# Moving three elementwise passes per image from VectorE to ScalarE in the convolution stage of a four-layer network

## What is computed

```python
# layer 0: five Newton-Schulz steps towards the inverse of every 128x128 channel image
x = x + _L0_conv_ref(_gn(x), 5)
# layer 1: 3x3 convolution of the quantised input
x = x + _L1_conv_ref(_gn(x), L1_conv_weight_int8, L1_conv_scale_weight, L1_conv_bias)
# layer 2: 5-tap diagonal convolution;  layer 3: 3x3 convolution on a torus
x = x + _L2_conv_ref(_gn(x), L2_conv_filter_w)
x = x + _L3_conv_ref(_gn(x), L3_conv_weight)

# the quantisation of layer 1
scale_input = jnp.max(jnp.abs(x_cl)) / 2.0 ** (ACTBIT - 1)
x_q = jnp.round(jnp.clip(x_cl / scale_input, -n, n))        # n = 127
```

## Time and profile before

| | us |
|---|---|
| median of 3 runs | 4286.94 |
| lowest and highest run | 4285.88 and 4287.16 |
| profiled execution: its span, first to last instruction | 4285.7 |
| start of the second stage's first matmul in that span | 2277.1 |

### The profile page before, as it was taken

How to read it: one execution, slowest core, us unless ns; L and a number is a source line. 1 busy time by engine, 2 the same in 40 slices (tenths; PEclk the granted TensorE clock), 3 DMA queues, 4 the chain that set the end, 5 groups by cost and what they waited for, 6 DMA issues and landing times. The chain is left out here.

```text
span 4285.7 us, 81705 instructions
## 1 busy us (share of the span) xinstructions
PE 4194.6 (98%) x30409; PEld 3108.7 (73%) x30409; DVE 3444.2 (80%) x7393; ACT 2072.5 (48%) x4296; POOL 2407.9 (56%) x3149
## 2 busy tenths in 40 slices
PE   7999999999999999999996999999999999999998
PEld 7999999999999999999992444444444444444443
DVE  6888888888888888888876787878787888888784
ACT  5776777777777777777761222222222222222221
POOL 6888888888888888888871222222222222222221
PEclk9999999999999999999997999999999999999999
DMA  2221222222222222222214555555555555555553
GB/s 69 64 62 55 65 65 60 60 60 60 60 66 65 60 63 68 60 60 60 60 41 97 133 137 134 137 133 137 134 138 134 138 134 138 134 138 134 138 134 84
DMA packets 333657, 404.28 MB, mean 94 GB/s; under 512 B 23088, under 2 KB 286032, under 8 KB 316880
## 3 DMA queue, kind: packets, MB, share of 16 engines
q1 hardware_dynamic: 308688, 334.25, 30.8%
q10 hardware_dynamic: 24576, 64.79, 5.6%
HBM read 135.22 MB, written 134.22 MB: 63 GB/s over the span
## 5 line engine op out<-in xcount | busy, mean ns | idle before, releaser
L1392 PE MATMUL bank<-xn,wt 128*128 128x512 f16 (+1 forms) x6912 | 1661.6, 381 | 19.9 <-issue 10.7
L1164 POOL TENSOR_TENSOR xn<-F,xn 128x512 f16<-128x512 f32 x512 | 541.6, 1090 | 1453.2 <-ACT xn L1202 1453.2
L1392 PEld LDWEIGHTS bank<-xn,wt 128*128 128x128 f16 (+1 forms) x6912 | 672.9, 100 | 805.0 <-issue 21.9
L463 ACT ACTIVATE P<-bank 128x512 f32<-128x512 f32 x1024 | 606.8, 608 | 264.0 <-PE bank L962 154.5
L1266 DVE SCALAR_TENSOR_TENSOR x<-bank,wu,x 128x512 f32<-128x512 f32 x512 | 382.4, 747 | 313.7 <-PE bank L1399 306.6
L1202 ACT ACTIVATE xn<-F 128x2048 f16<-128x2048 f32 x128 | 244.9, 1913 | 603.3 <-DVE F L1322 603.3
L1399 PE MATMUL bank<-xh,wth 96*128 96x512 f16 (+1 forms) x1792 | 515.6, 380 | 12.1 <-DMA xh<-xn 12.1
L313 POOL TENSOR_TENSOR W<-W 128x512 f16<-128x512 f32 x256 | 290.3, 1166 | 145.7 <-ACT W L489 145.7
L1277 DVE BATCH_NORM_STATS2 bs<-x 128x6 f32<-128x512 f32 x512 | 355.6, 695 | 17.7
L569 DVE BATCH_NORM_STATS2 st<-X 128x6 f32<-128x256 f32 x1024 | 351.5, 411 | 5.8 <-DMA X<-in_x 5.7
L1399 PEld LDWEIGHTS bank<-xh,wth 96*128 96x128 f16 (+1 forms) x1792 | 174.2, 97 | 232.6 <-DMA xh<-xn 15.7
(11 more groups left out here) (129 smaller groups left out, 7619.3 us busy)
## 6 DMA issues: line engine op xcount, KB each, us to landing
X<-in_x SPq DMA_DIRECT2D x64, 1024.0 KB, 4.8
x_scratch<-X SPq DMA_DIRECT2D x64, 1024.0 KB, 5.6
X<-x_scratch SPq DMA_DIRECT2D x64, 1024.0 KB, 8.8
out<-x SPq DMA_DIRECT2D x64, 1024.0 KB, 3.9
xh<-xn SPq DMA_DIRECT2D x384, 131.8 KB, 4.5
xh<-xn ACTq DMA_DIRECT2D x384, 131.8 KB, 5.4
xh<-xn SPq DMA_DIRECT2D x192, 65.9 KB, 3.2
xh<-xn ACTq DMA_DIRECT2D x192, 65.9 KB, 2.7
```

The source lines that it names most:

```text
L463: nc.scalar.activation(into[:, 4 * q:4 * q + 4, :], banks[q][:, :].rearrange("p (m w) -> p m w", m=4), ACT.Copy).then_inc(sb, 1)
L1164: ins = nc.gpsimd.tensor_tensor(padded(xn[l][odd], 1)[:, a + 1:a + 5, L:L + H], F[l][:, a:a + 4, :], padded(xn[l][odd], 0)[:, a + 1:a + 5, ...
L1392: nc.tensor.matmul(bank, wt[l][:, a, k, :], v, start=(k == a == b == 0), stop=False)
```

## The change

- F of layers 2 and 3 is computed by ACT (in `upper`, ahead of the f16 copy, on the same engine) as r * x + nb instead of by DVE as (x - m) * r. DVE computes the column nb = -m * r, of width 1, in `normalise`, and a new semaphore `scale_set` takes it to ACT. F -> copy is now a wait of ACT for itself.
- The first pass of the quantisation, T, is computed by ACT in a new function `quotients` as acol * x + ncol; DVE's `quantise` waits for it (semaphore `quotient`) and does the other two passes. `quotients(s+1)` stands in ACT's order behind `halos(3, s-2)` and ahead of `root(2, s)`.
- ncol = -mcol * acol is computed once, at the end of the first stage.

```diff
+ncol = persistent("ncol", [H, B])
...
 link.done(nc.vector.tensor_scalar(acol[:, :], acol[:, :], inv[:, 0:1], None, ALU.mult))
 link.wait()
+link.done(nc.vector.scalar_tensor_tensor(out=ncol[:, :], in0=mcol[:, :], scalar=-1.0, in1=acol[:, :],
+                                         op0=ALU.mult, op1=ALU.mult))
+link.wait()
...
+def quotients(n, h, odd):
+    act.wait_ge(x1_in[odd], 16 * h + 16)
+    need(act, normed[1], n)
+    nc.scalar.activation(T[:, :, :], xs[1][odd][:, :, :], ACT.Identity, scale=acol[:, n:n + 1],
+                         bias=ncol[:, n:n + 1]).then_inc(quotient, 1)
 def upper(l, n, odd):
+    act.wait_ge(scale_set[l], n + 1)
+    need(act, normed[l], n)
+    nc.scalar.activation(F[l][:, :, :], xs[l][odd][:, :, :], ACT.Identity, scale=cols[l]["r"][:, 0:1],
+                         bias=cols[l]["nb"][:, 0:1]).then_inc(scaled_f[l], 1)
     act.wait_ge(scaled_f[l], n + 1)
     nc.scalar.activation(padded(xn[l][odd], 0)[:, 1:NJ + 1, L:L + H], F[l][:, :, :],
                          ACT.Copy).then_inc(high[l], 1)
...
     halos(3, s - 2, odd)
+if there(s + 1):
+    quotients(s + 1, h + odd, 1 - odd)
 if there(s):
     root(2, s)
     upper(2, s, odd)
...
+quotients(0, 0, 0)
 first(0, 0, 0)
 run(act, step)
...
 def quantise(n, h, odd):
-    dve.wait_ge(x1_in[odd], 16 * h + 16)
-    link = Link(dve, q_chain, 2 * n)
-    link.done(nc.vector.tensor_scalar(T[:, :, :], xs[1][odd][:, :, :], mcol[:, bass.ds(n, 1)],
-                                      acol[:, bass.ds(n, 1)], ALU.subtract, ALU.mult))
-    link.wait()
+    dve.wait_ge(quotient, n + 1)
+    link = Link(dve, q_chain, n)
     link.done(nc.vector.tensor_scalar(T[:, :, :], T[:, :, :], QMAX, MAGIC, ALU.min, ALU.add))
...
 def normalise(l, n, odd):
-    need(dve, normed[l], n)
...
     link.done(nc.vector.tensor_tensor(c["r"][:, :], c["ra"][:, :], c["rb"][:, :], ALU.mult))
     link.wait()
-    nc.vector.tensor_scalar(F[l][:, :, :], xs[l][odd][:, :, :],
-                            c["m"][:, 0:1], c["r"][:, 0:1], ALU.subtract,
-                            ALU.mult).then_inc(scaled_f[l], 1)
+    nc.vector.tensor_scalar(c["nb"][:, :], c["r"][:, :], c["m"][:, 0:1], -1.0, ALU.mult,
+                            ALU.mult).then_inc(scale_set[l], 1)
```

More of the change, by code:

```diff
@@ L1077, in conv_net @@
             PART = 512 // 2
-            cols = [None, None] + [{k: sb(f"{k}{l}", [H, 1]) for k in ("m", "s", "q", "ve", "sd", "ra", "rb", "r")}
+            cols = [None, None] + [{k: sb(f"{k}{l}", [H, 1]) for k in ("m", "s", "q", "ve", "sd", "ra", "rb", "r", "nb")}
                                    for l in (2, 3)]
@@ L1087, in conv_net @@
             q_chain = sem("q_chain")
+            quotient = sem("quotient")
+            scale_set = [None, None] + [sem(f"scale_set{l}") for l in (2, 3)]
             biased = sem("biased")
```

## The result

| | before | changed |
|---|---|---|
| median, lowest to highest run, us | 4287.05, 4285.88 to 4288.18 (4 runs) | 4384.49, 4383.02 to 4385.93 (4 runs) |
| span of the profiled execution, us | 4285.7 | 4382.4 |

The change makes the kernel slower: the ratio is 1.0228, with a 95% interval from 1.0213 to 1.0242. The forecast was 4374 us, in a range from 4345 to 4405.

What follows compares the result with a forecast made beforehand. PE bound the old kernel at 30.525 us a step; the chain, grown to 31.96, becomes the bound: +1.43 over 61 steps is +87, span 4373, plus 1.2 gives 4374 us, range 4345 to 4405.

Steps and rivals of the forecast that it cites:

- the chain through ACT, POOL and DVE: Second stage's steady steps: image rounds chained through three engines, closing each step; 25.77 us before, 31.96 after, above PE's 29.97.
- Its length: Chain in a steady step: 18.76 us for the first half and 13.20 for the second, together 31.96 us.
- The issues as a part of the chain: ACT's queue in both halves: DMA issues hold ACT up, so 3.3 us of each `halos` belong to the chain.
- DVE's relief is all that counts: Rival: ACT computes while its queue issues DMAs, the chain loses up to 6.7 us; 4253 us at best; chance 0.04.
- PE's need: PE in a steady step: 30.525 us less its 0.55 wait for DVE's `s`, so 29.97 us.
- DVE's idle time for the quotient: Sign of being right: DVE idle about 3 us for the quotient, which starts as layer 3's halo issue ends.
- No fall of the clock: PE's steady steps: waits split into pieces of about 1 us keep the clock; rival, falling clock, 4682 us, chance 0.03.
- Halos in time: Layer 2's halos in steady steps: 7.5 us to issue and land, 8.2 to 9.6 available, so free.
- the 4.75 us of the chain: Steady step before the change: chain of 25.77 us in a step of 30.525, leaving 4.75 us to spare.

Runs made afterwards that it cites:

- quotient early: Changed kernel with the quotient of image s+2 moved behind `upper(3)`, where ACT waits for POOL: 4271.20 us, ratio 0.9962 to the kernel before.
- without the issues: Changed kernel with ScalarE's half of the `halos` DMAs issued from SyncE's queue: 4276.78 us, ratio 0.9976 to the kernel before.
- PE kept busy: Changed kernel with quotient done twice in place, plus 14 unread PE matmuls ahead of the wait for layer 3's `s`: 4520.27 us, against 4561.54 without them.

## Why the prediction was right, step by step

- *That the chain through ACT, POOL and DVE becomes the bound* was right. The trace shows it link by link, and three runs that shorten it in different ways (without the quotient, with the quotient early, without the issues) end at the same 4271 to 4277 us.
- *Its length*, forecast at 31.96 us, is 32.12; 0.16 us over 61 steps are the 10 us between forecast and result. Most of it is nb, the one width-1 column that DVE computes: from the reciprocal to F's start on ACT takes 1.21 us instead of 1.14, twice in a step, since nb takes 0.21 where a width-1 operation at 0.16 was assumed. Another 0.04 is the quotient's start, 3.42 behind the first issue where the root had 3.38. F and quotient were sized right: both have 2.09, for 2.10.
- *The issues as a part of the chain* was right, against the idle time that the list of waits puts down to `ve`: in the changed kernel both quotient and root follow the last issue by about 0.1 us, and in the kernel that issues from SyncE's queue the quotient stands 3.4 us nearer to `wrap`. The rival "DVE's relief is all that counts" became true there. It was described rightly, but its gain was priced too high: 4253 us at best, where the runs stop at 4271.
- *PE's need* was the term mis-sized in that price: 29.97 us, from the wait of 0.55 that the load engine shows. With no such wait left a step takes 30.19 (quotient early). The wait of the weight load, 0.55, held PE's stream up by only 0.33. The forecast does not suffer by it, since the chain, and not PE, sets its length.
- *A bound is missing from it.* The prediction compares the chain with PE's need alone. The kernel with only the quotient shows a third round, through PE, DVE's residuals and ACT, that is longer than both (30.98 us reckoned, against 30.1 and 30.2). In the changed kernel this round stays about 1.2 us short of the chain, the time for which DVE waits for ACT's root ahead of `normalise(3)` (1.18 and 1.23 in the rows above). That it did no harm here is luck: nothing in the prediction tests it.
- *DVE's idle time for the quotient* was given as about 3 us and is 4.89. The figure left the chain's new phase out; nothing else rested on it.
- *No fall of the clock*, at waits for both `s` of about 1 us each on the weight load, some 2 us a step as forecast, was right: 1.00 in the steady stretch. The rival was not empty, though: 2 us more in the chain call it up. There what the Trainium skill ("TensorE: Matmul & The Clock Gate", section "HAM oscillation — how this bites in real kernels") tells of a PE that waits between bursts agrees in kind with the trace, which shows the clock of 0.78 and 0.58 behind the wait; the waits that it tells of are longer than the 2.5 us here.
- *Halos in time*: of the 15.0 us for which PE waited for halos by the page, 1.4 lie between 2400 and 4280, so in the steady steps they stayed free.

## What to carry to other kernels

Before you move work to an idle engine, look for the place in its program: on an engine that works in order, with DMA issues and waits for others between its operations, a pass costs its full length if it stands on a chain that closes in each iteration and sets its pace, and nothing if it fills a wait for another engine. Add up the chain around one iteration, with DMA issues as busy time of the engine that issues them, and compare it with the bound engine's need; the difference is the most that may be added. Do the same for every other round that shares links with this chain: the quotient alone stayed within the 4.75 us of the chain and cost 27 us by the round through PE. Here the same three passes cost 97 us with the quotient in one place and gained 16 with it in the other, and the gain came from one of them alone, layer 3's F.

## What had not been expected of the hardware

Behind a wait of PE of some 2.5 us, in steps that are otherwise dense, the clock fell to the 1.2 GHz level again and again (0.94 over 200 us). In the changed kernel, whose waits on PE are 1.1 us at most, and with PE kept busy, where they are 0.8 on average and 1.8 at most, it stays at 1.00 in the rows above. Since PE had time to spare, a slower clock should have been hidden; it cost 0.72 us a step (34.94 against 34.22), because it fell just ahead of the residual on which the chain depends.

A multiplication over 8 columns of DVE (L1310, `deviations`) took 0.17 us in one half of the step and 1.12 in the other, in which POOL was at work on `lower`; it ended at 3434.03, POOL's work at 3434.01. That POOL held it up is not shown by a run of its own. Before the change the slow turn lay in layer 3's half (0.48 us, and 1.01 for the operation behind it). As PE's `var` waits for its result, that gave a new wait of PE's weight load for `q`, 0.56 us in each step.

```profile
3432.91 1.12 DVE L1310 TENSOR_TENSOR dv<-dv 128x8 f32<-128x8 f32 x1
```

```profile
PEld bank L1425 <- DVE q L1316: 32.9, 59, 0.6
```
